# Differential attention: key operand prepared once, mask added by TensorE, one exponential per map on ScalarE

## The reference, cut to what matters

```
q = rope((y @ Wq).reshape(B, T, 2*H, 8));  k = rope((y @ Wk).reshape(B, T, 2*8, 8))
s1 = q1 @ k1.T * 8**-0.5;   s2 = q2 @ k2.T * 8**-0.5        # per head, causal mask
attn = softmax(s1) @ v - lambda_full * (softmax(s2) @ v)    # v has 16 channels per kv head
attn = attn / sqrt(mean(attn**2) + 1e-6) * rms_w * (1 - LAMBDA_INIT)
x = x + attn.reshape(B, T, 256) @ Wo
```

## Time and profile before

| | |
|---|---|
| time, three runs | 2704.63, 2710.78 (median), 2714.89 us |
| the profiled execution's own time, and its span | 2712.94 us, 2711.2 us |
| busy in the span: TensorE matmul, VectorE, ScalarE, GpSimd | 2228.2, 1308.1, 956.8, 687.1 us |
| mean granted clock | 0.88 |
| scores of sequence 0 start; last `keep` starts | 2382.23 us; 2648.03 us |

### The profile page before, as it was taken

How to read it: one execution, slowest core, us unless ns; L and a number is a source line. 1 busy time by engine, 2 the same in 40 slices (tenths; PEclk the granted TensorE clock), 3 DMA queues, 4 the chain that set the end, 5 groups by cost and what they waited for, 6 DMA issues and landing times. The chain is left out here.

```text
span 2711.2 us, 59977 instructions
## 1 busy us (share of the span) xinstructions
PE 2228.2 (82%) x24624; PEld 1817.9 (67%) x24624; DVE 1308.1 (48%) x2900; ACT 956.8 (35%) x1689; POOL 687.1 (25%) x505
## 2 busy tenths in 40 slices
PE   5799999999999732869958999999999999844443
PEld 3677887888888611659946888888888888422223
DVE  3445454554545478231144545454545455344445
ACT  3244444444444232213232444444444444110001
POOL 3121222122121000100043443344434440033320
PEclk9799999999999675969987999999999999765557
DMA  4455555555554100143235555565565653000000
GB/s 116 112 132 127 136 128 138 124 126 136 130 130 105 44 21 0 35 144 109 79 100 131 137 141 140 137 141 139 138 143 141 142 122 79 18 0 0 0 0 22
DMA packets 166860, 267.45 MB, mean 99 GB/s; under 512 B 70713, under 2 KB 86210, under 8 KB 166594
## 3 DMA queue, kind: packets, MB, share of 16 engines
q1 hardware_dynamic: 166594, 263.66, 39.3%
HBM read 98.70 MB, written 1.05 MB: 37 GB/s over the span
## 5 line engine op out<-in xcount | busy, mean ns | idle before, releaser
L691 DVE CUSTOM_DVE_ANT_0 scores_d<-scores_d,mask_scaled_d 128x512 f32<-128x512 f32 (+1 forms) x512 | 281.4, 601 | 145.8 <-PE scores_d L536 142.8
L648 ACT ACTIVATE exp_d<-scoresT_d 128x512 f32<-128x512 f32 (+1 forms) x416 | 248.6, 598 | 274.2 <-PE scoresT_d L570 272.0
L695 DVE TENSOR_REDUCE max_parts_a<-scores_a 128x1 f32<-128x512 f32 (+1 forms) x512 | 263.6, 567 | 152.1 <-PE scores_a L536 152.1
L648 ACT ACTIVATE exp_a<-scoresT_a 128x512 f32<-128x512 f32 (+1 forms) x416 | 248.2, 597 | 210.5 <-PE scoresT_a L570 208.8
L570 PEld LDWEIGHTS scoresT_d<-q_stack_d,k_stack_d 128*128 128x128 f32 (+1 forms) x1664 | 244.8, 187 | 24.1
L570 PE MATMUL scoresT_a<-q_stack_a,k_stack_a 128*128 128x128 f32 (+1 forms) x1664 | 259.4, 281 | 0.9 <-DVE q_stack_a L712 0.9
L570 PEld LDWEIGHTS scoresT_a<-q_stack_a,k_stack_a 128*128 128x128 f32 (+1 forms) x1664 | 230.2, 195 | 28.0 <-issue 3.2
L570 PE MATMUL scoresT_d<-q_stack_d,k_stack_d 128*128 128x128 f32 (+1 forms) x1664 | 228.0, 260 | 0.0
L536 PE MATMUL scores_a<-k_stack_a,q_stack_a 96*128 96x512 f32 (+1 forms) x512 | 175.2, 395 | 42.7 <-DMA k_stack_a<-k_hi_a 20.7
L679 DVE SCALAR_TENSOR_TENSOR k_lo_d<-project_d,bk_d,k_hi_d 128x512 fp32r<-128x512 f32 (+1 forms) x128 | 81.0, 635 | 258.2 <-ACT k_hi_d L631 258.2
L679 DVE SCALAR_TENSOR_TENSOR k_lo_a<-project_a,bk_a,k_hi_a 128x512 fp32r<-128x512 f32 (+1 forms) x128 | 81.0, 635 | 253.5 <-ACT k_hi_a L631 253.4
(11 more groups left out here) (371 smaller groups left out, 4882.6 us busy)
## 6 DMA issues: line engine op xcount, KB each, us to landing
k_stack_a<-k_hi_a SPq DMA_DIRECT2D x256, 128.0 KB
k_stack_d<-k_hi_d SPq DMA_DIRECT2D x256, 128.0 KB
raw_a<-in_ctxT SPq DMA_DIRECT2D x48, 512.0 KB, 4.1
raw_d<-in_ctxT SPq DMA_DIRECT2D x48, 512.0 KB, 4.9
w_c<-in_L_ffn_W SPq DMA_DIRECT2D x23, 1024.0 KB, 8.7
k_stack_a<-k_hi_a SPq DMA_DIRECT2D x256, 72.2 KB, 2.1
k_stack_d<-k_hi_d SPq DMA_DIRECT2D x256, 72.2 KB
k_stack_a<-k_lo_a SPq DMA_DIRECT2D x128, 128.0 KB
```

What stands on the lines that cost most here:

```text
L648: nc.scalar.activation(eT[at % RING][0:r, :], ST[at % 2][0:r, :], ACT.Exp).then_inc(exp_done, 1)
L691: nc.vector.tensor_tensor_reduce(SC[at % 3][:, 0:w], SC[at % 3][:, 0:w], mf[m % 2][:, BANK * chunk:BANK * chunk + w], 1.0, NEG, ALU.add, A ...
L695: nc.vector.reduce_max(parts[:, j, chunk:chunk + 1], SC[at % 3][:, 0:w], AX.X).then_inc(score_free, 1)
```

## The change

- `k_block` is built for all sequences at once in the projection block, by two GpSimd products of 128x4096; it holds 8 units for each half of the rows, so that a scores matmul runs over 64 rows instead of 128. k is projected first, q afterwards, straight into the layout that `scores` reads. v is masked on its way out of PSUM, by VectorE. `q_now` and `v_now` are gone.
- The causal mask is a matmul of its own, in float32r, into the same PSUM bank as the scores.
- The maximum is taken by VectorE out of PSUM and negated; ScalarE takes the exponential of each of the 16 units by itself, out of PSUM, with scale, its own bias and its own sum (`accum_out`): 16 instructions of 64 columns for one of 1024.
- `weigh` works with the ratio of the two sums: the second map is multiplied (512 columns) and added to the first; the reciprocal of the first sum is applied in `keep`. `move` goes from ScalarE to VectorE.
- The squares and the gain are done per sequence by GpSimd, the sums of squares per four sequences by VectorE in the loop; the block behind it loses them and works in four parts.
- The loop is written out for 16 sequences.

```diff
@@ differential_stage, projection block
+                for i in range(2):
+                    pool.wait_ge(rotated, i + 1)
+                    nc.gpsimd.tensor_tensor(
+                        kb[:, 8 * i:8 * i + 8, :, :],
+                        kT[:, BANK * i:BANK * i + BANK].rearrange("p (b u t) -> p b u t", u=1, t=T)
+                        .to_broadcast([P, 8, 8, T]),
...
+                nc.vector.tensor_copy(eye[:, :], chip.ident)
+                nc.vector.tensor_copy(causal[:, :, :], chip.cst("causal").rearrange("p (o t) -> p o t", o=1)
+                                      .to_broadcast([P, KV, T]))
...
+                    nc.vector.tensor_tensor(v[:, 4 * i:4 * i + 4, :], pj[4 + i][:, :].rearrange("p (a c) -> p a c", c=P),
+                                            chip.cst("row_half_of_head").rearrange("p (a c) -> p a c", a=1)
...
@@ causal_maps
         def _(pool):
+            for b in range(NB):
+                pool.wait_ge(kept, b + 1)
+                nc.gpsimd.tensor_tensor(sq[:, b, :], heads[:, b, :], heads[:, b, :], ALU.mult).then_inc(squared, 1)
...
-            def scores(b, par):
-                pe.wait_ge(blocks_ready, b + 1)
-                after(pe, taken, b - 1)
+            def scores(b):
+                after(pe, exp_done, b - 1)
                 for i in range(2):
+                    bank = ps[b % 2][:, BANK * i:BANK * i + BANK]
+                    nc.tensor.matmul(bank, eye[:, :], causal[:, :, :].rearrange("p u t -> p (u t)"),
+                                     start=True, stop=False, skip_group_check=True)
+                    rows = slice(64 * i, 64 * i + 64)
+                    ins = nc.tensor.matmul(bank, q[rows, b, :, :].rearrange("p r t -> p (r t)"),
+                                           kb[rows, b, :, :].rearrange("p u t -> p (u t)"),
+                                           start=False, stop=True, skip_group_check=True)
...
+            for b in range(NB):
+                act.wait_ge(maxed, b + 1)
+                after(act, diffed, b - 1)
+                for u in range(U):
+                    ins = nc.scalar.activation(sc[b % 2][:, u, :], ps[b % 2][:, T * u:T * u + T], ACT.Exp, scale=SCALE,
+                                               bias=mx[:, b % 2, u:u + 1], accum_out=sm[:, b % 2, u:u + 1])
+                ins.then_inc(exp_done, 1)
...
+            largest(0)
+            for b in range(NB):
+                if b:
+                    if b >= 2:
+                        keep(b - 2)
+                    weigh(b - 1)
+                if b + 1 < NB:
+                    largest(b + 1)
+                if b:
+                    move(b - 1)
+                if b % 4 == 3 and b > 4:
+                    squares(b // 4 - 1)
```

More of the change, by code:

```diff
@@ L1441, in _ @@
                 for i in range(3):
-                    for q in range(2):
+                    for part in range(2):
                         for sw in range(2):
-                            bank = (4 * i + 2 * q + sw) % 8
+                            bank = (4 * i + 2 * part + sw) % 8
                             if i == 2:
-                                pe.wait_ge(rotated, q + 1)
-                            w = wq[:, :, D * sw + P * i:D * sw + P * i + P] if i < 2 else wk[:, :, P * sw:P * sw + P]
+                                pe.wait_ge(rotated, part + 1)
+                            w = wk[:, :, P * sw:P * sw + P] if i == 0 else wq[:, :, D * sw + P * i - P:D * sw + P * i]
                             for c in range(HALVES):
-                                ins = nc.tensor.matmul(pj[bank][:, :], w[:, c, :], yT[:, c, BANK * q:BANK * q + BANK],
+                                ins = nc.tensor.matmul(pj[bank][:, :], w[:, c, :], yT[:, c, BANK * part:BANK * part + BANK],
                                                        start=c == 0, stop=c == 1)
@@ L1468, in _ @@
                 nc.vector.tensor_reduce(ls[:, 0:2], lp[:, :, :], AX.X, ALU.add).then_inc(lam_in, 1)
+                nc.vector.tensor_copy(eye[:, :], chip.ident)
+                nc.vector.tensor_copy(causal[:, :, :], chip.cst("causal").rearrange("p (o t) -> p o t", o=1)
+                                      .to_broadcast([P, KV, T]))
+                link(nc.vector.tensor_scalar(gain[:, :], gain[:, :], 1.0 - LAMBDA_INIT, None, ALU.mult))
                 for i in range(3):
-                    for q in range(2):
-                        bank = (4 * i + 2 * q) % 8
-                        dve.wait_ge(projected, 2 * i + q + 1)
-                        after(dve, rotated, 2 * i + q)
+                    for part in range(2):
+                        bank = (4 * i + 2 * part) % 8
+                        dve.wait_ge(projected, 2 * i + part + 1)
+                        after(dve, rotated, 2 * i + part)
                         for sw, table in enumerate(("cos", "sin")):
@@ L1640, in _ @@
-            bodies(pe, body)
-            values(NB - 1, 1)
+            scores(0)
+            for b in range(NB):
+                if b + 1 < NB:
+                    scores(b + 1)
+                if b:
+                    values(b - 1)
+            values(NB - 1)
         @block.scalar
         def _(act):
-            def move(b, par):
-                act.wait_ge(turned, b + 1)
-                nc.scalar.activation(dT[par][:, :, :], pt[par][:, :].rearrange("p (a c) -> p a c", c=P),
-                                     ACT.Copy).then_inc(moved, 1)
@@ L1695, in _ @@
-            bodies(dve, body)
-            keep(NB - 2, 0)
-            weigh(NB - 1, 1)
-            keep(NB - 1, 1)
+                sums, inverse = [t[:, b % 2, :].rearrange("p (k m) -> p k m", m=2) for t in (sm, rc)]
+                maps = sc[b % 2][:, :, :].rearrange("p (k m) t -> p k m t", m=2)
+                step(nc.vector.reciprocal(rc[:, b % 2, :], sm[:, b % 2, :]), 1)
+                step(nc.vector.scalar_tensor_tensor(ratio[:, b % 2, :], inverse[:, :, 1], minus_lam[:, :], sums[:, :, 0],
+                                                    ALU.mult, ALU.mult), 2)
@@ new lines, in weigh, with move @@
+                step(nc.vector.tensor_tensor(diff[b % 2][:, :, :], maps[:, :, 1, :], wide(ratio[:, b % 2, :]),
+                                             ALU.mult), 3)
+                nc.vector.tensor_tensor(diff[b % 2][:, :, :], maps[:, :, 0, :], diff[b % 2][:, :, :],
+                                        ALU.add).then_inc(diffed, 1)
+            def move(b):
+                dve.wait_ge(turned, b + 1)
+                after(dve, valued, b - 1)
+                nc.vector.tensor_copy(dT[b % 2][:, :, :], pt[b % 2][:, :].rearrange("p (a c) -> p a c", c=P)
+                                      ).then_inc(moved, 1)
@@ new lines, in _ @@
+            largest(0)
+            for b in range(NB):
+                if b:
+                    if b >= 2:
+                        keep(b - 2)
+                    weigh(b - 1)
+                if b + 1 < NB:
+                    largest(b + 1)
+                if b:
+                    move(b - 1)
+                if b % 4 == 3 and b > 4:
+                    squares(b // 4 - 1)
+            keep(NB - 2)
+            weigh(NB - 1)
+            move(NB - 1)
+            keep(NB - 1)
+            squares(3)
```

179 lines of the change are left out of this document (66 added, 113 removed).

## The result

The changed kernel took 2586.25 us (median of four runs, 2583.07 to 2588.26) against 2707.70 us for the one before (four runs, 2695.89 to 2714.89): a ratio of 0.9554, interval [0.9517, 0.9592]. The prediction was 2587. The profiled execution took 2587.63 us (before 2712.94), with a span of 2585.8.

The account below looks back on a forecast made before the run. No engine is full; a chain across engines in stage E's loop bounds it. Projection block +1.0, loop -117.6 and block behind -7.1 sum to -123.7 from the profiled 2712.94 us: 2589.2, so a median of 2587 us, range 2552 to 2606.

Parts of the forecast that it names:

- The turn: Loop of stage E: scores, maximum, negation, move and values form a ring of 8.70 us; thirteen make 113.1.
- the price of the scores: Loop, TensorE: masks and half-row products priced by columns alone, 2 x (0.43 + 1.71) + 0.37 + 0.04 = 4.69 us.
- To scores(2): Start of the loop, from the first scores: scores(0) 3.6, maximum and negation 1.5, exponentials 6.0; scores(2) starts at 11.1 us.
- the tail: End of the loop, from scores(15) on: its turn 8.7, then steps without overlap, 14.0 for sequences 14 and 15, and last sums.
- the block behind: Block after the loop: 8.1 us instead of 15.2, a change of -7.1 us.
- The projection block: Block ahead of the loop: VectorE's second and third rotation adds wait out GpSimd's 6.8 us products; first scores +1.0 us.
- the forecast's own: Range of the main case, clock low and exponentials hidden: 2578 to 2597 us, chance 0.50.
- Full clock: Rival for the loop: TensorE, busier, runs at 2.4 GHz; 2552 us, or 2585 with exponentials of 8.5; chance 0.25.
- the ring that the rival named: Loop at full clock: `keep`, `weigh`, maximum, negation, move and values in a row, 6.4 us a turn.
- ScalarE bounds: Rival for the loop: sixteen exponentials over 8.6 us set the turn; 2603 us at 9.5, 2617 at 10.5; chance 0.17.
- slower: Rival: ScalarE alone sets the loop, gain gone at 1.01 us an exponential, 2760 us at 1.2; chance 0.02.
- Port: Rival for the loop: GpSimd's products block `weigh` out of its cover; 2602 us if every turn lost 1; chance 0.06.

Follow-up runs that it names:

- the second experiment: Changed kernel with the score products over all 128 rows, q stored twice with the other half's rows zero; 2569.13 us.
- the fourth experiment: Changed kernel with the mask's operands in float32 instead of float32r, still over 128 rows; 2631.77 us.
- the ninth experiment: Changed kernel with GpSimd's two key products of 4096 columns written as eight of 1024; 2592.65 us.
- the fifth experiment: Changed kernel with both mask products first, then both half products, over the same rows; 2546.58 us.
- the tenth: Changed kernel with masks over 64 rows and TensorE's and VectorE's orders rewritten (transposes of b, scores of b+2, values of b); 2558.60 us.
- The seventh experiment: Changed kernel with each sequence's sixteen exponentials done twice, the first sixteen into spare tiles; 2595.75 us.
- The third experiment: Changed kernel with the two mask products left out, so later keys are attended to as well; 2552.13 us.
- first: Changed kernel with the mask products over the 64 rows of their half instead of 128; 2555.42 us.
- eleventh: Changed kernel with TensorE's and VectorE's orders rewritten, masks and score products over all 128 rows, the other half's queries zero; 2587.16 us.

## Why the prediction was right, and where it was right by luck

The mechanism held. The total is closer than its terms deserve: stage E lost 113.7 us (from its projection block on) where 123.7 was summed, and the missing 10.0 us was made up by stages A to D, 11.6 us shorter in this profile up to that point.

**The turn**, 8.70 predicted, 9.36 measured. The step that failed is the price of the scores, 4.69 us predicted against 5.54 measured (mask at 2448.05 to maximum at 2453.59): the sentence "I take the columns as what counts". The columns were right (0.43 and 1.71), but each change between 128 and 64 rows costs 0.29 us: the two between the half products make 0.59 of the 0.85, and the first mask 0.28, half of which the second experiment has without a change too. That it is the rows is shown by the fourth experiment (one type, still 0.29) and the second (one row count, 0.59 gone). In the trace the next weights' load starts only with the product where the rows change; that this load is what fills the 0.29 fits its length, and no run tests it by itself. The negation cost 0.09 instead of 0.21, since the move doesn't wait for its end, and the move 0.74 instead of 0.81. Thirteen turns: 121.6 against 113.1, **+8.5** of the missing 10.0.

**The ends.** To scores(2) 10.45 (11.1), since sixteen exponentials took 4.85 us and not 6.0, inside the bounds of 3.5 and 8.5; the tail 23.8 (24.3); the block behind 7.9 (8.1). **-1.3** together. The projection block came out +1.5 (+1.0). The wait is as foreseen, the second and third add ending just behind GpSimd's products, and the ninth experiment confirms it. But the size is luck: at the clock of 1.00 that the block had before, it takes 31.6 us against 31.5, +0.1, and the other 1.4 are its start at a clock of 0.50 in this profile. The Trainium skill, SBUF — State Buffer, section SBUF: two separate sides, calls the shared pair an exclusive lock for the whole instruction; the trace agrees, with an add of 6.15 us beside a product of 7.08 and at most 2.32 beside pieces of 1.90 to 2.36.

**Not foreseen:** the output stage's first products took 9.44 us, where before they took 7.17, **+2.3**. In the ninth run they took 7.17 with the same code in that stage, at a clock of 1.00; in the changed kernel the mean was 0.76. The end of the loop was at 0.50 in each. It isn't a mark of the change, since four of the fourteen profiles have the 7.17 and one of them is the kernel before; what decides it is open.

**The stages ahead.** They are the same code, and their end scatters over 16 us in fourteen profiles. For the two kernels of the comparison the profile shows where they differ (5.9 us by the end of stage A, 5.6 in D). The four times of the changed kernel are within 5.2 us of each other, and whether its stages ahead were short in all four is not known: only one was profiled. With those stages as long as in the profile of before, its profiled execution would have taken 2599.2 us (2587.63 + 11.6): still inside the whole range of 2552 to 2606, but above the forecast's own of 2578 to 2597. (The terms given for that range make 2594 at its upper end: 2587 + 2.5 + 1.5 + 3.) So, as far as the one profile shows, the hit within 1 us is luck: two errors of some ten us cancel.

**Full clock** (0.25) didn't come; the clock was 0.50 from 2373.84 on, through the whole loop. The reason given, products over 64 rows, is borne out in part: with only their rows filled to 128 the clock was 0.77. It isn't the whole of it, since the fifth experiment (the same rows in another order) and the tenth (all of the scores over 64 rows) had turns well above 0.50. The estimate of that rival, 2552, is about what narrow masks gave (2555.42), mostly at 0.50: the ring that the rival named, `keep` to values, then bounds the turn, because the scores got shorter and not the clock higher.

**ScalarE bounds** (0.17), **slower** (0.02): 0.30 us for one exponential with its sum, 4.85 of 9.36. The seventh experiment puts the edge at twice the work. The page of the Trainium skill named in the prediction, ScalarE: Activation LUTs, gave an estimate of 3.9 us for the sixteen, "silent on the sum". The trace has 4.85 us: it shows the sum read as an instruction of its own, and pairs 0.29 us apart.

**Port** (0.06): beside GpSimd's product with the gain (2449.01 to 2449.47) one product of `weigh` took 0.90 us instead of 0.69 (2449.10), under the scores with 2.86 us to spare.

**What I didn't look for.** Two products over different halves of the rows can run at the same time. The prediction asked only whether half the rows shorten one product, and no row of stage E in the kernel before shows the rest. The Trainium skill, TensorE: Matmul & The Clock Gate, Part 3: Packing small matmuls — row/col tiling, says that products in different row groups run concurrently. The third experiment agrees: four records in 2.08 us where two took 2.07. With the masks out of their way the scores were 2.3 us shorter (fifth experiment) and, masks side by side too, 2.9 (first). The kernel as changed lost 44 us there by the middle part (164.4 against 119.9), 46 by the stage's length.

## What to carry to other kernels

Where a ring across engines bounds a loop, write the ring down and time each member; sums by engine told nothing in the tenth and eleventh experiments, and doubling the work of an engine outside the ring cost 0.10 us a turn. Two products that use different halves of the rows should stand next to each other, with nothing of another row count between: moving a cheap 128-row product (0.43 us) out from between them was worth 2.3 us a turn. Judge a change of one stage by that stage's length; the total carries the scatter of all others, here as large as the error it hid. Within the stage, look at the clock of the parts that the change doesn't touch: two of them together moved by up to 3.7 us from one profile to another.

## What the runs showed of the hardware that was not expected

- A change of row count between two neighbouring products at a clock of 0.50 costs 0.29 us in both directions: 2.00 from start to start for 1.71 of columns, with operands of one type or of two. The load of the next weights, 0.29 us, then starts only with the product (2450.76), and 0.42 us ahead of it where the row count stays (2447.53 for 2447.95).
- Products over rows 0 to 63 and 64 to 127 overlap fully (2.08 us for four records), and a 128-row product between them prevents it.
- TensorE can be busy 44.62 of 50 us at a clock of 0.50, as in the changed kernel. With only the score products' rows filled to 128 the mean was 0.77 at 38.43 busy. Half rows do not fix it: all scores over 64 rows, it was 0.50 at 39.38 busy (third experiment) and 0.60 at 36.16 (tenth).
- An exponential with `accum_out` is two instructions on ScalarE, a pair of them each 0.29 us at 64 columns. Back to back with 32 in a row, the view by line shows 1.16 us as the median of one exponential, though the pairs start 0.29 to 0.30 apart: durations there overlap, and only the spacing tells the price.
